# Transposing x and the quantized tiles by DMA instead of on TensorE, in a fused retention and fp4-linear kernel

## What is computed

```
xn  = layernorm(x)
q,k,v = heads(xn @ Wq + bq) / 8, heads(xn @ Wk + bk), heads(xn @ Wv + bv)
ret = (q @ k.T) * D                  # D[i,j] = exp(decay * (i-j)), causal
ret = ret / clip(|rowsum(ret)|, 1)
g   = groupnorm(ret @ v) * gn_w + gn_b
att = (silu(xn @ Wg + bg) * g) @ Wo + bo
ffn = fp4_quantize(xn) @ fp4_quantize(Wf).T * scales + bias   # blocks of 16
out = x + att + ffn
```

## Time and profile before

| | |
|---|---|
| median of 3 runs | 2420.5 us (2419.79 to 2421.73) |
| span of the profiled execution | 2417.8 us |
| PE busy | 2210.8 us, 91% |
| DVE busy | 1531.9 us, 63% |
| ACT, POOL busy | 597.0 us and 564.8 us |
| DMA queue of SP | 242.58 MB, 29.8% of the 16 engines' span |
| one MIDDLE body | 67.7 us (parity 1), 24 of them |

### The profile page before, as it was taken

One profiled execution on the slowest core, in us unless ns is written; L12 is line 12 of the kernel. 1 busy time (PEld: TensorE's weight loads), 2 busy tenths in 40 slices (PEclk: granted clock), 3 DMA queues, 4 the chain that ended last, 5 costly groups with the idle time before them and its releaser, 6 DMA issues.

```text
span 2417.8 us, 42345 instructions
## 1 busy us (share of the span) xinstructions
PE 2210.8 (91%) x13548; PEld 1194.2 (49%) x13600; DVE 1531.9 (63%) x3894; ACT 597.0 (25%) x883; POOL 564.8 (23%) x428
## 2 busy tenths in 40 slices
PE   1289898888889999999989999999989999999999
PEld 1145454444445555555545555555545555555553
DVE  7766677779775565656664565666664656666642
ACT  5533232222222222222222222222212222222210
POOL 1022221222122222222222222222222222222221
PEclk9689999999999999999999999999999999999999
DMA  7953232222222222222222222222222222222223
GB/s 283 365 183 117 76 101 92 91 69 82 95 79 87 87 68 89 97 88 86 87 76 83 78 78 95 96 87 87 87 71 76 72 95 95 87 87 87 87 70 113
DMA packets 79572, 243.44 MB, mean 101 GB/s; under 512 B 8592, under 2 KB 29584, under 8 KB 78480
## 3 DMA queue, kind: packets, MB, share of 16 engines
q1 hardware_dynamic: 79504, 242.58, 29.8%
HBM read 202.71 MB, written 37.75 MB: 99 GB/s over the span
## 4 chain that ended last, share of the span: by engine, by line
PE 75%; DVE 14%; issue 4%; ACT 2%; DMA 2%; SPq 2%; POOL 1%; DVEq 0%; ACTq 0%; POOLq 0%
PE mm L1099 46%; PE mm L1064 11%; PE four L1152 4%; PE mm L1075 4%; PE four L1147 2%; PE tp L1109 2%; PE four L1119 2%; PE tp L1131 2%; PE tp L1038 1%; SPq L270 1%; PE tp L1161 1%; DVE xa L706 1%; DVE xa L711 1%; DVE xa L712 1%; DVE xa L707 1%
## 5 line engine op out<-in xcount | busy, mean ns | idle before, releaser
L1099 PE MATMUL mm<-xnT,wring 128*128 128x512 f16 x6144 | 1385.5, 384 | 34.4 <-issue 14.0
L1099 PEld LDWEIGHTS mm<-xnT,wring 128*128 128x128 f16 x6144 | 601.1, 99 | 744.5 <-issue 53.6
L1064 PE MATMUL mm<-wo,yT 128*128 128x512 f16 x1536 | 342.3, 379 | 0.6 <-POOL yT L422 0.6
L1064 PEld LDWEIGHTS mm<-wo,yT 128*128 x1536 | 148.3, 99 | 170.8 <-issue 1.1
L419 POOL TENSOR_TENSOR yT<-attn,gate 128x512 f32 x64 | 83.6, 1306 | 591.2 <-ACT attn L582 562.5
L401 POOL TENSOR_TENSOR qparts<-qT,qparts 128x512 f16<-128x512 f32 x64 | 76.2, 1190 | 616.9 <-ACT qT L554 616.9
L897 DVE TENSOR_TENSOR probs<-four,dmask 128x512 f32<-128x512 f32 x128 | 82.4, 685 | 215.0 <-PE four L1119 213.7
L401 POOL TENSOR_TENSOR kparts<-kT,kparts 128x512 f16<-128x512 f32 x64 | 76.0, 1187 | 422.9 <-ACT kT L554 407.7
L929 DVE TENSOR_REDUCE gs<-attn 128x8 f32<-128x512 f32 x64 | 43.9, 686 | 175.1 <-ACT attn L568 175.1
L552 ACT ACTIVATE kparts<-mm,bias,cols 128x512 f16<-128x512 f32 x64 | 49.8, 778 | 340.3 <-PE mm L1099 190.0
L674 DVE BATCH_NORM_STATS2 ls<-xt 128x6 f32<-128x512 f32 x64 | 41.2, 685 | 135.7 <-DMA xt<-in_x 135.2
(11 more groups left out here) (167 smaller groups left out, 2505.0 us busy)
## 6 DMA issues: line engine op xcount, KB each, us to landing
wring<-parts SPq DMA_DIRECT2D x256, 512.0 KB, 3.3
xt<-in_x SPq DMA_DIRECT2D x33, 512.0 KB, 3.5
out<-res SPq DMA_DIRECT2D x32, 512.0 KB, 2.7
res<-in_x SPq DMA_DIRECT2D x28, 512.0 KB, 4.4
parts<-xqT SPq DMA_DIRECT2D x36, 256.0 KB, 4.4
parts<-xnT SPq DMA_DIRECT2D x36, 256.0 KB, 3.3
res<-in_w_f SPq DMA_DIRECT2D x16, 512.0 KB, 3.4
yT<-in_w_k SPq DMA_DIRECT2D x1, 4096.0 KB, 14.6
```

The source lines that it names most:

```text
L1064: last = MM(mm[0][:], y[:, yj, k, ds(q * P, P)], wo[:, wj, k, h * GROUP:(h + 1) * GROUP], start=(n == 0), stop=(n == 3 * KT - 1))
L1099: last = MM(mm[n % 2][:], wring[:, n, wj, k, :], xnT[:, parity, xj, k, :], start=(j == 0), stop=(j == 3 * KT - 1))
```

## The change

- `xt` is split in the token layout: ACT writes the f16 high half of the whole 128 x 1024 tile to a new buffer `xhl` (`x_hi`, between its second and third evacuation of a body, after a wait for `xn_ready`), POOL subtracts it for the low half (`x_lo`, right behind `decay_q(0)`).
- SP issues transposing DMAs of 256 KB each, SBUF to SBUF: the two halves into `xnT` (`move_x_parts`), and `xq` into `xqT` (`move_x`) or `wf` (`move_xq`). The `t1_full` waits of DVE before it writes `xq` again become waits for `xq_moved`, and so does the one ahead of `finish_linear`.
- TensorE's transposes L1038 (but for START's) and L1046, ACT's copies L475 and L481 and DVE's L722, L730 and L734 are gone from the bodies. `load_x` doesn't wait for `t0_full` any more. In SECOND the weight slices 1 to 3 of pair 0 are issued behind the wait for the first quantized weight tile.
- One constant (`identb`) is not loaded; `ident`, the f32 one, stays.

The table of event counts (`PER`) and the order of the PSUM banks (`bank_uses`) follow these edits and are not shown. The lines on SP, POOL, ACT, DVE and PE:

```diff
@@ SP @@
                 def load_x():
+                    if (phase, i) == (FIRST_A, 0):
+                        w("t0_full", 0)
                     w("xq_ready", 0)
-                    w("t0_full", 0)
                     sp.dma_start(xt[:], a["x"][ds(group * GROUP + GROUP + q * P, P), :])\
                       .then_inc(s["x_loaded"], 16)
+                def move_xq(k, dst):
+                    w("xq_ready", k)
+                    sp.dma_start(dst, xq[:], transpose=True).then_inc(s["xq_moved"], 16)
+                def move_x_parts():
+                    w("xlo_ready", 1)
+                    for j in range(2):
+                        sp.dma_start(xnT[:, 1 - parity, j, :, ds(q * P, P)], xhl[:, j, :], transpose=True)\
+                          .then_inc(s["x_moved"], 16)
+                def move_x():
+                    move_xq(2 if phase == SECOND else 1,
+                            xqT[:, 1 - parity, ds(q, 1)].rearrange("p a k t -> p (a k) t"))
...
                 if phase == SECOND:
                     w("f_max", 0)
                     load_res(f_rows[0])
-                    load_slices(0)
-                    w("xq_ready", 1)
+                    load_slices(0, (0,))
+                    move_xq(1, wf[:, :, ds(q * (2 * P), P)])
                     load_res(f_rows[1])
-                    load_slices(1)
-                    w("xq_ready", 3)
+                    load_slices(0, (1, 2, 3))
+                    move_x_parts()
+                    load_slices(1, (0, 1))
+                    move_x()
+                    load_slices(1, (2, 3))
+                    move_xq(3, wf[:, :, ds(q * (2 * P) + P, P)])
                     load_res(a["x"][rows, :])
                 else:
                     w("xq_ready", 0)
                     load_res(a["x"][rows, :])
                     load_slices(0)
+                    move_x_parts()
                     load_slices(1)
                 w("out_ready", 1)
                 sp.dma_start(a["out"][rows, :], res[:]).then_inc(s["out_stored"], 16)
+                if phase == MIDDLE:
+                    move_x()
@@ POOL @@
+                def x_lo():
+                    w("xhi_ready", 1)
+                    nc.gpsimd.tensor_tensor(xhl[:, 1], xt[:], xhl[:, 0], ALU.subtract).then_inc(s["xlo_ready"], 1)
...
                 decay_q(0)
+                x_lo()
                 split(3, kT, kparts)
@@ ACT @@
+                def x_hi():
+                    w("x_moved", 0)
+                    w("xn_ready", 1)
+                    nc.scalar.activation(xhl[:, 0], xt[:], ACT.Copy).then_inc(s["xhi_ready"], 1)
...
                 evacuate(0, 1)
+                x_hi()
                 evacuate(0, 2)
@@ DVE @@
-                    w("t1_full", 0)
+                    w("xq_moved", 0)
...
-                w("t1_full", uses["f0"][1] if phase == SECOND else 0)
+                w("xq_moved", 1 if phase == SECOND else 0)
...
-                x_lo(w, 1 - parity, q, *uses["x0"], 0, 1)
-                x_lo_last(w, 1 - parity, q, uses["x1"][0], 2, 1)
@@ PE @@
                 w(f"{name}_free", before + h)
+                w("xq_moved", 0)
...
-                w("xn_ready", 1)
-                transpose_x(w, *uses["x0"], 0)
-                transpose_x(w, *uses["x1"], HK)
                 attend(1)
...
-                if phase == SECOND:
-                    transpose_xq(w, *uses["f1"], 3)
-                else:
-                    transpose_xq(w, *uses["xq"], 1)
                 transpose_g(1)
```

More of the change, by code:

```diff
@@ L597, in body @@
                     evacuate(0, 3)
-                if phase == SECOND:
-                    store_f(0)
                 if phase == FIRST_B:
@@ L612, in body @@
                 copy_v(1)
-                if phase == SECOND:
-                    store_xq()
                 if phase not in FIRST:
@@ L621, in body @@
                     evacuate(0, 3)
-                if phase in FIRST:
-                    for h in range(2):
-                        act.wait_ge(stored[h], 16 * 4 * (PAIRS + 1))
-                copy_x_hi(w, 1 - parity, q, *uses["x0"], 0)
-                copy_x_hi(w, 1 - parity, q, *uses["x1"], HK)
                 copy_attn(1)
@@ L982, in body @@
                     emit_out(w, 0, 4, linear)
-                if phase in FIRST:
-                    for h in range(2):
-                        dve.wait_ge(stored[h], 16 * 4 * (PAIRS + 1))
-                x_lo(w, 1 - parity, q, *uses["x0"], 0, 1)
-                x_lo_last(w, 1 - parity, q, uses["x1"][0], 2, 1)
                 group_norm(1)
@@ L1040, in transpose_x @@
                 last.then_inc(s[f"t{bk}_full"], 1)
-            def transpose_xq(w, bk, use, ready):
-                w("xq_ready", ready)
-                w(f"t{bk}_free", use - 1)
-                for k in range(KT):
-                    last = nc.tensor.transpose(tp[bk][:].bitcast(BF16)[:, k * P:(k + 1) * P],
-                                               xq[:, k * P:(k + 1) * P], identb[:])
-                last.then_inc(s[f"t{bk}_full"], 1)
             pe.wait_ge(const_in, 16 * NCONST)
@@ L1259 @@
     }
-    nc = bacc.Bacc("TRN2", target_bir_lowering=False, num_devices=1)
+    nc = bacc.Bacc("TRN2", target_bir_lowering=False, num_devices=1, dynamic_dma_scratch_size=1024)
     a = {}
```

45 lines of the change are left out of this document (14 added, 31 removed), and 4 rows, old and new, of the table PER.

## The result

| | before | changed |
|---|---|---|
| median of 18 runs (range) | 2420.7 us (2418.3 to 2426.3) | 2426.8 us (2415.3 to 2440.4) |
| ratio, 95% interval | | 1.0027 (1.0016 to 1.0038) |
| span of the profiled execution | 2417.8 us | 2424.7 us |

The forecast was 2443 us, +22; measured are +6. The side is right and the time lies in the range, but the size is off by a factor of almost four. The terms of the prediction are used throughout: d is what the extra step of SP's queue costs DVE, c what `x_lo` costs it, the mark is the 3.35 us of delay at which the carry copies (L912 of before) run into POOL's `split` and `add_biases`, and a body in which they do is said to collide. The two profiled spans (+6.9 us) are close enough to the medians (+6.1) that the place of the difference can be read from them. I measured each body from start to start of its second `transpose_g`.

What follows compares the result with a forecast made beforehand. TensorE's work was taken to bound MIDDLE, DVE SECOND. Terms -10.6 + 15.8 + 8 + 7 - 1 - 0.5 + 3.7 = +22.4 us on the median 2420.5 gave 2443 us, range 2400 to 2466 (8 in 10).

Steps and rivals of the forecast that it cites:

- d: At the body's start, one more DMA on SP's queue ahead of the load of xt: 1.4 us, bounds 0.35 and 9.3.
- c: In MIDDLE, DVE's quantizing steps stretched beside POOL's x_lo: 2.6 us, bounds 1.8 and 3.1.
- the mark: In parity-1 bodies, 3.35 us of delay, beyond which L912 no longer ends before POOL's L401 begins.
- What bounds a body: MIDDLE: TensorE's work, with a DVE chain at the body's end; 0.88 us of transposes won, the other 0.45 worth nothing.
- The collision: Parity-1 MIDDLE bodies: L912 held by POOL, attend(0) 2.2 us late; +1.3 net in each of 12, together +15.8 us.
- The three quarters behind c: DVE beside POOL loses three quarters of POOL's time, from 0.84 + 0.95 of 2.4 us: 3.6 us, less 1.0 already paid.
- rival 1: MIDDLE: d + c stays under 3.35 us, so L912 is clear of POOL; 2408.5 us, chance 0.23.
- The clock: Behind the new wait at attend(0), a lower granted clock: 1.4 us in half of 12 bodies, +8, bounds 0 and 20.
- SECOND: Four bodies bound by DVE: 0.9 us of transposes won, x_lo costs 2.2, weight tile wait 0.5; +7, bounds -4 and +12.
- TAIL: First finish_linear waits 4.2 us more for the last move_x, some 0.5 of it spent waiting anyway: +3.7 us.
- START and FIRST: START: one constant less, -0.5 us; FIRST: four times -0.88 against x_lo in the late body, -1, bounds -4 and +4.
- rivals 3 and 4: Transposing DMAs hold queue or engines longer: 2468 us at d = 4, chance 0.10; 2570 us at 9.3 us each, chance 0.05.

Runs made afterwards that it cites:

- the run with xq alone: The kernel before with, in MIDDLE alone, xq transposed by a DMA behind the out store and x left on TensorE; 2424.9 us, ratio 1.0017.
- the run with more d: The changed kernel plus a second transposing DMA of xq into a dump tile behind move_x in MIDDLE; 2486.4 us, ratio 1.0269.
- the run with both edits: The kernel before plus, in MIDDLE, a dead transposing DMA behind the out store and a dead POOL subtraction behind decay_q(0); 2454.5 us, ratio 1.0147.
- the best kernel here: The kernel before with x alone moved by DMAs in MIDDLE, x_lo behind add_biases, plus 22 unread matmuls in SECOND; 2386.1 us, ratio 0.9867.

## Where the prediction was right, and the step that failed

- **What bounds a body: right.** Parity 0 went from 67.25 to 66.37 us, the 0.88 of `transpose_x`, and parity 1 from 67.7 to 66.85. That xq's 0.45 us are worth nothing was a claim about a chain through four engines, and the run with xq alone bore it out.
- **The collision: right in its place and first price, wrong in how often.** L912 held by POOL's pair, 2.2 us at `attend(0)`, parity 1 alone: all measured. The failed step is the sum d + c = 4.0 us, taken for all 12 bodies: it measured 2.7 to 3.0 and so stayed under its own mark of 3.35 in 9 of them, and 4.8 in the 3 that collided. The text called the mark 0.65 us away and each term known to about 1 us, and gave the other side 0.23, but one value of the sum should not have carried 12 bodies. Within it, d was sound (the load goes out 1.4 us later) and c mis-sized: 2.6, measured 1.8 by itself, because a step that reads PSUM or is under way is not stretched. The three quarters behind c also took 2.4 us for two POOL instructions that last 1.16 and 1.48; with 2.64 they are two thirds, and c would have been 2.3.
- **What I missed about the mark** is that bodies are not alike, and that the delay jumps by 1 us when POOL's `split` gets ahead of one DVE step. The first body of each group is late by almost 2 us more (1.1 at DVE's start, 0.9 of stretching). So the true picture lay between the forecast and rival 1: three collisions. The side came out right by them alone: with `x_lo` later and no collision the kernel takes 2411.3 us, faster than before.
- **The clock: wrong in size.** I counted 1.4 us in half of the cases. In the changed kernel it is 3.5 us in all three. In the other runs it is nothing or about 3.5 (bodies longer by 2.2 to 2.8, or by 5.5 to 6), with 1.9 and 5.2 once each in the run with more d, and the length of the wait doesn't tell which: behind the 1.97 to 1.99 us of the run with both edits it is 0.3 us five times and 3.5 or 3.6 four times. The twelve of the run with more d cost 70 us together, where the forecast had 12 x 2.2 + 8 = 34 (14 us of the 70 are the three waits of 4.4 to 4.9). Two errors, too many collisions and too cheap ones, partly cancelled.
- **SECOND: right in its main term, the rest by luck.** +1.8 a body was made of 2.2 for `x_lo` beside DVE (measured 1.8), 0.5 for the wait on the move of f0 (zero: it landed 1.3 us early) and -0.9 for the transposes. The last was not won: from `attend(1)` to `finish_half(1)` pass 5.20 us in the body shown, 4.05 before, because that stretch now runs at a clock of 0.50 (0.63 before). The weight slices, priced at zero, cost 4.86 us of waiting, which didn't matter as such. That the transposes had kept the clock up by breaking up the wait is argued; what is shown is that matmuls put into it hold the clock, worth 4.4 us over the four bodies of the changed kernel.
- **TAIL: right**, +4.4 for +3.7. The wait is 3.6 us longer (5.16 for 1.52); the rest is part of what the clock costs, L1077 at 3.59 us against 1.90 behind this wait:

```profile
2347.22 3.59 PE L1077 MATMUL tp<-wf,xqT 128*128 128x512 bf16 x8 [5.16 <-DMA xqT<-xq]
```

- **START and FIRST**: -1.5 forecast, +2.7 measured, 2.4 of it ahead of the end of the first body. Kernels with START and FIRST as before reach that point between 175.99 and 178.69 us, before itself at 176.66, the changed one at 179.05. Most of it can be scatter; it stays open.
- **Unforeseen: -6.0 us** where MIDDLE's loop jumps back from a parity-1 group to parity 0 (below). It belongs to no term of the sum, which took all 24 bodies for bound by TensorE's work; these two take 75.9 and 76.2 us before, with TensorE idle for over 6.
- **The DMAs**: rivals 3 and 4 are out. The row agrees with the Trainium skill, "Advanced Engine Details and Errata", section "X-Bar Transpose (TRN2)" (as fast as regular ones): 3.0 us to landing for 256 KB. The 1309 ns for each 128x128 tile in "VectorE: DVE Perf Modes", section "The three transpose paths", would be 10.5 us for such a move, an estimate from that page; the measurement decides, it is 3.0.

## What to carry to other kernels

When a change moves work off the bounding engine onto others that had slack, price it by its distance to the next thing that it runs into, body by body, and treat a margin smaller than your error as two cases: here some 0.4 us of slack decided between 0 and 5.7 us, 12 times over. Delays on two engines that exclude each other add up only if the order in which they start stays the same: here one order gave 3.0 us and the other 4.1, so measure them together, in more than one body. And before you take work from an engine that waits a lot, ask what that work did in the gaps: a TensorE that waited 2.0 to 2.6 us paid for it again in the matmuls behind the wait in 18 of 30 such cases here, and filler matmuls in a longer wait, with the part of the change that pays, make the best kernel here.
